# First steps of a LoRA feed-forward: high products ahead, gated rows in halves, A_down last

## The chip, the cores and the metric

The kernel runs on one core of a Trainium2 chip. The metric is the device time of one execution in microseconds (us). The core has five engines with queues of their own: TensorE (PE in the rows; PEld is its weight load), VectorE (DVE), ScalarE (ACT), GpSimd (POOL) and SyncE (SP, which here only issues DMAs). They meet through semaphores: an instruction raises one when it is done (`then_inc`), another waits until it has a value (`wait_ge`). Each queue runs in order, so an instruction that waits holds all behind it.

## The reference

For x of 32 sequences x 32 tokens x 512 the program computes two layers, each a "conditioner" and a feed-forward, with a residual:

```python
# layer 0, per sequence b with its expert id itok_B_2_6[b]
gate = x @ W_gate.T + 0.5 * (x @ A_gate[id].T) @ B_gate[id].T       # F = 1376, rank 16
up   = x @ W_up.T   + 0.5 * (x @ A_up[id].T)   @ B_up[id].T
act  = silu(gate) * up
down = act @ W_down.T + 0.5 * (act @ A_down[id].T) @ B_down[id].T    # back to 512
W_eff = U_top*relu(S_top*alpha+beta) @ Vh_top + U_tail*S_tail @ Vh_tail + U_r*S_r*relu(D) @ R @ Vh_r
x = x + down @ W_eff.T + bias
# layer 1: router over 8 experts, rank-16 LoRA of the top two, then an int8-like feed-forward
x = x + ffn_quantized(base(x) + 2 * lora_top2(x))
```

Only layer 0, up to its second feed-forward step, is touched.

## The kernel before

**Two numbers for one.** A float32 matmul is made of three products of rounded parts. Each operand is split in a high copy (`_hl[..., HI]`, a rounding copy on ScalarE, L559) and a low rest (raw minus high, a subtraction on VectorE, L907). TensorE then adds high x high, high x low and low x high in PSUM: `THREE`, L58. So every operand passes ScalarE, then VectorE, then TensorE.

**Steps.** The tokens are two halves (n = 0, 1) of 512. The 1376 rows of the hidden size are 11 tiles of 128, so layer 0 has 22 steps s = 11 n + f. A step is `gate_up` (L1337): 12 matmuls for gate, 6 of LoRA with B, 12 for up, 6 of LoRA; then silu on ScalarE (L645), times up on VectorE (L998, `act_raw`), the split of it (`act_hl`), and `down` (L1351): 6 matmuls with A_down (L1362) into the bank TD, 12 with W_down (L1369) into the banks 0 to 3. TensorE runs `gate_up(s + 1)` before `down(s)`.

**The first 44 us.** TensorE's order is written out (L1386 to L1413): warm-up, two of four effective-weight blocks (`w_eff`, L1299), a small product of the mix matrix (L1398, result `ps[TD]`, which ScalarE and VectorE copy to `c_hl`), step 0's 24 base matmuls for gate and up (L1326), `w_eff(2)`, x times the gathered A rows (`lora_in`, L1317), `w_eff(3)`, `delta` (L1308, reads `c_hl`), step 0's LoRA products with B (L1332), step 1's `gate_up`, step 0's `down`, step 2. The result of `lora_in` is masked so that each sequence keeps its own expert's rows (VectorE, four instructions at L977, to `tg_tmp`; the first two are the gate part, the last two the up part) and split to `tg_hl`; the LoRA products read that.

**The other queues.** ScalarE and VectorE go through the same steps, in `step` (L653, L1018): split the next step's gate/up weights and B rows, silu or product, then A_down (`ad_hl`), W_down (`wd_hl`) and `act_hl`. The A and B rows of a sequence's expert come by gathers that GpSimd issues one after the other (L472, L485), from a list that starts at once: A of gate and up, B of steps 0 and 1, A_down (L510), B of step 2, and so on. SyncE loads the rest; a buffer of weights is loaded again when both of its copies have been made (`load_wg`, L306; `load_wd`, L312), and these loads stand in order in one queue.

## Time and profile before

| | |
|---|---|
| median of 3 runs | 400.32 us (399.73 to 400.45) |
| profiled execution | 400.79 us |
| its span (first to last instruction) | 397.9 us |
| TensorE busy | 381.5 us, 96% |
| VectorE, ScalarE, GpSimd busy | 251.2, 187.7, 140.5 us |
| TensorE's granted clock | 0.9 or more of full speed in 39 of 40 slices |

The table says which engine is busiest over the whole span. It is an average: what an edit in the first tenth is worth is read from who waits for whom there, in the timelines of each engine, and from whether an engine waits later on.

### The profile page before, as it was taken

How to read it: one execution, taken by the hardware profiler on the slowest of the kernel's cores; microseconds unless marked ns; L12 is line 12 of the kernel's file. 1: busy time of each engine (PE TensorE's matmuls, PEld its weight loads, DVE VectorE, ACT ScalarE, POOL GpSimd, SP SyncE). 2: the span in 40 equal slices, each digit the busy share in tenths (PEclk: the TensorE clock that was granted, in tenths of full speed). 3: DMA queues.
4: the chain of work that ended last, by engine and by line, in shares of the span. 5: the costliest groups of instructions: out<-in, count | busy, mean ns of one | idle time of the engine just before them, and what ended most of it. 6: DMA issues, size and time to landing. Idle time of an engine off the chain costs nothing.

```text
span 397.9 us, 5993 instructions
## 1 busy us (share of the span) xinstructions
PE 381.5 (96%) x2029; PEld 302.9 (76%) x2029; DVE 251.2 (63%) x484; ACT 187.7 (47%) x313; POOL 140.5 (35%) x139
## 2 busy tenths in 40 slices
PE   7998999999999999999999999999989999999982
PEld 4687888888888988888888888889868874444442
DVE  5875844444454346756776666755574878989882
ACT  5544634333333244423454444642564547575760
POOL 2787877777301052200111130000000112757561
PEclk9999999999999999999999999999999999999998
DMA  7876644545333223732997796566378100113332
GB/s 285 283 229 239 212 138 146 160 158 161 115 105 105 81 79 110 238 112 92 311 284 210 204 234 162 106 107 224 126 186 203 73 0 2 37 44 93 89 90 80
DMA packets 48773, 58.84 MB, mean 148 GB/s; under 512 B 30305, under 2 KB 33147, under 8 KB 48623
## 3 DMA queue, kind: packets, MB, share of 16 engines
q1 hardware_dynamic: 43703, 47.15, 41.0%
q0 software_dynamic: 4320, 10.49, 8.6%
q10 hardware_dynamic: 728, 0.93, 0.7%
q8 instruction: 11, 0.18, 0.2%
q14 instruction: 11, 0.09, 0.1%
HBM read 50.02 MB, written 2.11 MB: 131 GB/s over the span
## 4 chain that ended last, share of the span: by engine, by line
PE 69%; DVE 12%; POOL 5%; ACT 5%; DMA 4%; issue 4%; SPq 0%; DVEq 0%; POOLq 0%; ACTq 0%
PE ps L1326 27%; PE ps L1369 15%; PE ps L1332 7%; PE ps L1484 5%; PE ps L1362 4%; PE ps L1438 3%; DVE hqs L1232 3%; ACT h_rnd L843 2%; DVE u_sb L1226 2%; POOL agu L472 2%; DVE g_sb L1223 2%; PE ps L1456 2%; PE ps L1379 1%; PE ps L1491 1%; DMA b_raw<-b_gu_dram,idx_all 1%
## 5 line engine op out<-in xcount | busy, mean ns | idle before, releaser
L1326 PE MATMUL ps<-x_hl,wg_hl 128*128 128x512 f32 x528 | 127.5, 391 | 0.7 <-DVE wg_hl L907 0.7
L1326 PEld LDWEIGHTS ps<-x_hl,wg_hl 128*128 128x128 f32 x528 | 97.6, 188 | 21.2 <-DVE wg_hl L907 1.6
L485 POOL DMA_INDIRECT b_raw<-b_gu_dram,idx_all x44 | 43.7, 994 | 95.5 <-DVE b_hl L907 84.9
L1369 PE MATMUL ps<-act_hl,wd_hl 128*128 128x512 f32 x264 | 64.0, 391 | 0.0
L1369 PEld LDWEIGHTS ps<-act_hl,wd_hl 128*128 128x128 f32 x264 | 48.2, 188 | 9.1
L998 DVE TENSOR_TENSOR act_raw<-ps,sil 128x512 f32<-128x512 f32 x22 | 15.2, 689 | 61.5 <-issue 37.3
L1332 PEld LDWEIGHTS ps<-tg_hl,b_hl 128*128 128x128 f32 x264 | 37.2, 190 | 4.5 <-issue 1.2
L1332 PE MATMUL ps<-tg_hl,b_hl 128*128 128x256 f32 x264 | 38.4, 282 | 0.8 <-DVE tg_hl L907 0.8
L527 POOL TENSOR_TENSOR qs<-qs,half 128x1 f32<-128x1 f32 x8 | 4.4, 551 | 89.0 <-DVE qs L1196 89.0
L559 ACT ACTIVATE act_hl<-act_raw 128x512 fp32r<-128x512 f32 x22 | 13.9, 632 | 44.8 <-DVE act_raw L998 44.8
L907 DVE TENSOR_TENSOR wg_hl<-wg_raw,wg_hl 128x1024 fp32r<-128x1024 f32 x22 | 26.9, 1224 | 12.6 <-ACT wg_hl L559 11.8
L536 POOL TENSOR_TENSOR g_sb<-g_sb,u_sb 128x459 f32<-128x459 f32 (+1 forms) x24 | 27.4, 1163 | 20.3 <-ACT g_sb L836 20.3
L691 ACT ACTIVATE nat<-nat,winv 128x512 f32<-128x512 f32 x22 | 14.7, 716 | 35.9 <-DVE winv L1010 35.9
L472 POOL DMA_INDIRECT agu<-a_gu_dram,idx_a x23 | 26.9, 1170 | 12.7 <-issue 6.7
L645 ACT ACTIVATE sil<-ps 128x512 f32<-128x512 f32 x22 | 12.9, 587 | 31.6 <-PE ps L1332 31.6
L472 POOL DMA_INDIRECT ad_raw<-a_d_dram,idx_a x24 | 25.0, 1040 | 7.3 <-issue 7.0
L1484 PE MATMUL ps<-wc_lo_hi,x_hl 128*128 128x512 f32 x96 | 23.8, 396 | 0.0
L1573 PE MATMUL ps<-wq_g,qt 128*128 128x459 bf16 (+1 forms) x96 | 22.6, 357 | 0.9 <-DVE g_sb L1223 0.9
L559 ACT ACTIVATE wg_hl<-wg_raw 128x1024 fp32r<-128x1024 f32 x22 | 23.0, 1045 | 0.2 <-DMA wg_raw<-w_gu_dram 0.2
L1438 PE MATMUL ps<-y_hl,we_hl 128*128 128x512 f32 x96 | 23.1, 394 | 0.0
L1573 PE MATMUL ps<-wq_u,qt 128*128 128x459 bf16 (+1 forms) x96 | 22.6, 358 | 0.0
L1362 PE MATMUL ps<-act_hl,ad_hl 128*128 128x256 f32 x132 | 19.6, 285 | 1.3 <-DVE act_hl L907 1.3
(173 smaller groups left out, 586.7 us busy)
## 6 DMA issues: line engine op xcount, KB each, us to landing
wg_raw<-w_gu_dram SPq DMA_DIRECT2D x22, 512.0 KB, 4.0
wd_raw<-w_d_dram SPq DMA_DIRECT2D x22, 256.0 KB, 2.7
nat<-w_nat_dram SPq DMA_DIRECT2D x11, 512.0 KB, 4.9
wdx<-w_nat_dram SPq DMA_DIRECT2D x11, 256.0 KB, 2.7
natd<-wd_nat_dram SPq DMA_DIRECT2D x4, 704.0 KB, 5.0
out_dram<-r_sb SPq DMA_DIRECT2D x7, 256.0 KB, 2.0
vu_raw<-w_vu_dram SPq DMA_DIRECT2D x3, 512.0 KB, 9.2
ws_b<-scale_scratch SPq DMA_DIRECT2D x2, 688.0 KB, 5.6
```

The costliest lines, as they stand in the source:

```text
L472: gp.indirect_dma_start(out=tile[:, b, :], out_offset=None, in_=a[table].rearrange("e p c -> (e p) c"), in_offset=bass.IndirectOffsetOnAxi ...
L485: gp.indirect_dma_start(out=b_raw[:, slot, g, :], out_offset=None, in_=a["b_gu"], in_offset=bass.IndirectOffsetOnAxis(ap=idx_all[:, f, 2 * ...
L536: nc.gpsimd.tensor_tensor(g_sb[:, slot, cols], g_sb[:, slot, cols], u_sb[:, slot, cols], ALU.mult).then_inc(h_made, 1)
L559: return nc.scalar.activation(o, i, ACT.Copy)
L907: return V.tensor_tensor(o, raw, hf(hi), ALU.subtract)
L1326: mm(bank[:], wg_hl[:, slot, w, gu * H + k * P:gu * H + (k + 1) * P], x_hl[n][:, v, k, :], start=(k == 0 and (w, v) == THREE[0]), stop=False)
L1332: last = mm(bank[:, g * GT:(g + 1) * GT], b_hl[:, slot, w, g, gu * P:(gu + 1) * P], tg_hl[:, n, v, gu, g * GT:(g + 1) * GT], start=False, ...
L1362: mm(ps[TD][:, g * GT:(g + 1) * GT], ad_hl[:, slot, w, g * P:(g + 1) * P], act_hl[:, slot, v, g * GT:(g + 1) * GT], start=(first and g == ...
L1369: last = mm(ps[m][:], wd_hl[:, slot, w, m * P:(m + 1) * P], act_hl[:, slot, v, :], start=(first and (w, v) == THREE[0]), stop=False)
L1438: last = mm(ps[m][:], we_hl[:, w, k, m * P:(m + 1) * P], y_of[n][:, v, k, :], start=(k == 0 and (w, v) == THREE[0]), stop=(k == KT - 1 and ...
L1484: mm(ps[CB[t]][:], x_hl[t // 4][:, w, k, (t % 4) * P:(t % 4 + 1) * P], wc_hl[v][:, k, :], start=(k == 0 and (w, v) == THREE[0]), stop=False)
L1573: last = mm(ps[(G_BANK, U_BANK)[gu][c]][:, 0:CH[c]], qt[:, t, k, :], wq(gu, k, slice(CO[c], CO[c] + CH[c])), start=(k == 0), stop=(k == KT ...
```

## The change

Three edits, all in the first two steps. TensorE does step 0's eight high x high products ahead of the mix product, and the other sixteen behind it. The split of the gated rows (`tg_hl`) is done in a gate half and an up half, on ScalarE and VectorE, with a count on the semaphores of two for each n; VectorE's split of step 1's weights goes behind it. In step 0 the split of A_down and its six matmuls go behind those of act and W_down.

```diff
             def tg_split(n):
-                act.wait_ge(tg_masked, 4 * (n + 1))
-                copy(tg_hl[:, n, HI], tg_tmp[:]).then_inc(tg_hi, 1)
+                for gu in range(2):
+                    act.wait_ge(tg_masked, 4 * n + 2 * gu + 2)
+                    copy(tg_hl[:, n, HI, gu], tg_tmp[:, gu]).then_inc(tg_hi, 1)
...
 
                 if not (isinstance(s, int) and s < 2):
                     act.wait_ge(down_done, s - 1)
-                ad_split(s, slot, f, n)
+                if not ad_behind:
+                    ad_split(s, slot, f, n)
                 wd_split(s, slot)
                 act_split(s, slot)
+                if ad_behind:
+                    act.wait_ge(ad_sp, 16 * AD_SP)
+                    act.wait_ge(ad_in[0], 16 * (HB - AD_SP))
+                    ad_split(s, slot, f, n)
 
             def bd_split(n):
...
-            act.wait_ge(ad_sp, 16 * AD_SP)
-            act.wait_ge(ad_in[0], 16 * (HB - AD_SP))
-            step(0, 0, 0, split_next=False, gate=False)
+            step(0, 0, 0, split_next=False, gate=False, ad_behind=True)
             step(1, 1, 0)
...
-                if n == 0:
-                    wg_split(1, 1)
-                dve.wait_ge(tg_masked, 4 * (n + 1))
-                dve.wait_ge(tg_hi, n + 1)
-                lo(tg_hl[:, n, LO], tg_tmp[:], tg_hl[:, n, HI]).then_inc(tg_lo, 1)
+                for gu in range(2):
+                    dve.wait_ge(tg_masked, 4 * n + 2 * gu + 2)
+                    dve.wait_ge(tg_hi, 2 * n + gu + 1)
+                    lo(tg_hl[:, n, LO, gu], tg_tmp[:, gu], tg_hl[:, n, HI, gu]).then_inc(tg_lo, 1)
 
             tg_split(0)
+            wg_split(1, 1)
             b_split(1, 1)
             for i in range(KT):
                 dve.wait_ge(we_hi, i + 1)
...
+            def ad_split(s, slot, f, n):
+                dve.wait_ge(ad_hi, s + 1)
+                lo(ad_hl[:, slot, LO, :].rearrange("p (b r) -> p b r", b=HB),
+                   ad_raw[:, n * HB:(n + 1) * HB, ds(f * RANK, RANK)],
+                   ad_hl[:, slot, HI, :].rearrange("p (b r) -> p b r", b=HB)).then_inc(ad_lo, 1)
+
+            def step(f, par, n, split_next=True, weights=True, ad_behind=False):
                 s, slot = n * FT + f, (n + par) % 2
                 if split_next:
                     wg_split(s + 1, 1 - slot)
                     b_split(s + 1, 1 - slot)
                 make_act(s, slot)
-                dve.wait_ge(ad_hi, s + 1)
-                lo(ad_hl[:, slot, LO, :].rearrange("p (b r) -> p b r", b=HB),
-                   ad_raw[:, n * HB:(n + 1) * HB, ds(f * RANK, RANK)],
-                   ad_hl[:, slot, HI, :].rearrange("p (b r) -> p b r", b=HB)).then_inc(ad_lo, 1)
+                if not ad_behind:
+                    ad_split(s, slot, f, n)
                 dve.wait_ge(wd_hi, s + 1)
                 lo(wd_hl[:, slot, LO, :], wd_raw[:, slot, :], wd_hl[:, slot, HI, :]).then_inc(wd_lo, 1)
                 dve.wait_ge(act_hi, s + 1)
                 lo(act_hl[:, slot, LO, :], act_raw[:], act_hl[:, slot, HI, :]).then_inc(act_lo, 1)
+                if ad_behind:
+                    ad_split(s, slot, f, n)
                 if n == 1 and weights and not (isinstance(f, int) and f < 2):
                     wq_max(f, par)
                     wq_round(f - 1, 1 - par)
@@ -1050,7 +1060,7 @@
                     dve.wait_ge(y_hi, KT * n + m + 1)
                     lo(y_of[n][:, LO, m, :], ps[m][:], y_of[n][:, HI, m, :]).then_inc(y_lo, 1)
 
-            step(0, 0, 0, split_next=False)
...
-            def gate_up_base(bank, slot, n, gu, first=False):
+            def gate_up_base(bank, slot, n, gu, first=False, terms=THREE):
                 for k in range(KT):
                     if first and k % 2 == 0:
                         pe.wait_ge(x_lo, k // 2 + 1)
-                    for w, v in THREE:
+                    for w, v in terms:
                         mm(bank[:], wg_hl[:, slot, w, gu * H + k * P:gu * H + (k + 1) * P], x_hl[n][:, v, k, :],
                            start=(k == 0 and (w, v) == THREE[0]), stop=False)
 
@@ -1341,15 +1351,24 @@
                 gate_up_base(ps[GATE], slot, n, 0)
                 pe.wait_ge(b_lo, s + 1)
                 if first:
-                    pe.wait_ge(tg_lo, n + 1)
+                    pe.wait_ge(tg_lo, 2 * (n + 1))
                 gate_up_lora(ps[GATE], slot, n, 0)
                 if not (isinstance(s, int) and s < 2):
                     pe.wait_ge(act_made, s - 1)
                 gate_up_base(ps[UP[slot]], slot, n, 1)
                 gate_up_lora(ps[UP[slot]], slot, n, 1)
 
+            def down_lora(s, slot, first, end):
+                pe.wait_ge(ad_lo, s + 1)
+                for g in range(2):
+                    for w, v in THREE:
+                        last = mm(ps[TD][:, g * GT:(g + 1) * GT], ad_hl[:, slot, w, g * P:(g + 1) * P],
+                                  act_hl[:, slot, v, g * GT:(g + 1) * GT], start=(first and g == 0 and (w, v) == THREE[0]),
+                                  stop=(end and g == 1 and (w, v) == THREE[-1]), skip_group_check=True)
+                return last
+
             def down(s, slot, n, first=False, end=False):
-                pe.wait_ge(ad_lo, s + 1)
+                lora_behind = first and not n
                 pe.wait_ge(wd_lo, s + 1)
                 pe.wait_ge(act_lo, s + 1)
                 if first:
@@ -1357,17 +1376,16 @@
                         pe.wait_ge(td_masked, n)
                     else:
                         pe.wait_ge(we_lo, KT)
-                for g in range(2):
-                    for w, v in THREE:
-                        mm(ps[TD][:, g * GT:(g + 1) * GT], ad_hl[:, slot, w, g * P:(g + 1) * P],
-                           act_hl[:, slot, v, g * GT:(g + 1) * GT], start=(first and g == 0 and (w, v) == THREE[0]),
-                           stop=(end and g == 1 and (w, v) == THREE[-1]), skip_group_check=True)
+                if not lora_behind:
+                    down_lora(s, slot, first, end)
                 for m in range(KT):
                     if first and n:
                         pe.wait_ge(x1_made, m + 1)
                     for w, v in THREE:
                         last = mm(ps[m][:], wd_hl[:, slot, w, m * P:(m + 1) * P], act_hl[:, slot, v, :],
                                   start=(first and (w, v) == THREE[0]), stop=False)
+                if lora_behind:
+                    last = down_lora(s, slot, first, end)
                 last.then_inc(down_done, 1)
 
             def lora_down(n):
@@ -1394,11 +1412,15 @@
             w_eff(0)
             w_eff(1)
 
+            pe.wait_ge(wg_hi, STEP0_TURN)
+            pe.wait_ge(x_hi, 2)
+            for gu, bank in ((0, ps[GATE]), (1, ps[UP[0]])):
+                gate_up_base(bank, 0, 0, gu, terms=THREE[0:1])
             pe.wait_ge(urs_ready, 1)
             mm(ps[TD][0:4, :], smalls[0:4, s_at["r"]], ur[:], start=True, stop=True).then_inc(cmix_ready, 1)
             pe.wait_ge(wg_lo, STEP0_TURN)
-            gate_up_base(ps[GATE], 0, 0, 0, first=True)
-            gate_up_base(ps[UP[0]], 0, 0, 1)
+            gate_up_base(ps[GATE], 0, 0, 0, first=True, terms=THREE[1:])
+            gate_up_base(ps[UP[0]], 0, 0, 1, terms=THREE[1:])
             w_eff(2)
             lora_in(0)
             w_eff(3)
@@ -1406,6 +1428,7 @@
             pe.wait_ge(b_lo, 1)
             pe.wait_ge(tg_lo, 1)
             gate_up_lora(ps[GATE], 0, 0, 0)
+            pe.wait_ge(tg_lo, 2)
             gate_up_lora(ps[UP[0]], 0, 0, 1)
             gate_up(1, 1, 0)
             down(0, 0, 0, first=True)
```

On TensorE, step 0's base matmuls (`x_hl` with `wg_hl`) around the mix product (`ur` with `consts`), before:

```order
L1398 MATMUL ps<-ur,consts 4x512 [waits urs_ready]
L1326 MATMUL ps<-x_hl_49,wg_hl 128x512 [waits x_lo,wg_lo]
L1326 MATMUL ps<-x_hl_49,wg_hl 128x512 x5
L1326 MATMUL ps<-x_hl_49,wg_hl 128x512 [waits x_lo]
L1326 MATMUL ps<-x_hl_49,wg_hl 128x512 x17
```

and now:

```order
L1336 MATMUL ps<-x_hl_49,wg_hl 128x512 [waits x_hi,wg_hi]
L1336 MATMUL ps<-x_hl_49,wg_hl 128x512 x7
L1420 MATMUL ps<-ur,consts 4x512 [waits urs_ready]
L1336 MATMUL ps<-x_hl_49,wg_hl 128x512 [waits x_lo,wg_lo]
L1336 MATMUL ps<-x_hl_49,wg_hl 128x512 x3
L1336 MATMUL ps<-x_hl_49,wg_hl 128x512 [waits x_lo]
L1336 MATMUL ps<-x_hl_49,wg_hl 128x512 x11
```

Eight of the 24 moved ahead of the mix product; they wait for the high copies alone. The same engine further on, from step 1's last LoRA products to step 2's first matmuls, before:

```order
L1332 MATMUL ps<-tg_hl,b_hl 128x256 x6
L1362 MATMUL ps<-act_hl,ad_hl 128x256 [waits act_lo,we_lo,wd_lo,ad_lo]
L1362 MATMUL ps<-act_hl,ad_hl 128x256 x5
L1369 MATMUL ps<-act_hl,wd_hl 128x512 x12
L1326 MATMUL ps<-x_hl_49,wg_hl 128x512 [waits silu_done,wg_lo]
```

and now:

```order
L1342 MATMUL ps<-tg_hl,b_hl 128x256 x6
L1385 MATMUL ps<-act_hl,wd_hl 128x512 [waits we_lo,act_lo,wd_lo]
L1385 MATMUL ps<-act_hl,wd_hl 128x512 x11
L1365 MATMUL ps<-act_hl,ad_hl 128x256 [waits ad_lo]
L1365 MATMUL ps<-act_hl,ad_hl 128x256 x5
L1336 MATMUL ps<-x_hl_49,wg_hl 128x512 [waits silu_done,wg_lo]
```

The wait for `ad_lo` now stands behind the twelve W_down matmuls. ScalarE, from the gated rows' copy to silu of step 1, before:

```order
L559 ACTIVATE tg_hl<-tg_tmp 128x1024 [waits tg_masked]
L559 ACTIVATE b_hl<-b_raw 128x512 [waits b_in1]
L645 ACTIVATE sil<-ps 128x512 [waits gate_ready]
L559 ACTIVATE we_hl<-ps 128x512 [waits we_ready] x4
L559 ACTIVATE ad_hl<-ad_raw 128x256 [waits ad_in0,ad_sp]
L559 ACTIVATE wd_hl<-wd_raw 128x512 [waits wd_in0]
L559 ACTIVATE act_hl<-act_raw 128x512 [waits act_made]
L559 ACTIVATE wg_hl<-wg_raw 128x1024 [waits wg_used,wg_in0]
L559 ACTIVATE b_hl<-b_raw 128x512 [waits b_in0]
L645 ACTIVATE sil<-ps 128x512 [waits act_made,gate_ready]
```

and now:

```order
L559 ACTIVATE tg_hl<-tg_tmp 128x512 [waits tg_masked] x2
L559 ACTIVATE b_hl<-b_raw 128x512 [waits b_in1]
L646 ACTIVATE sil<-ps 128x512 [waits gate_ready]
L559 ACTIVATE we_hl<-ps 128x512 [waits we_ready] x4
L559 ACTIVATE wd_hl<-wd_raw 128x512 [waits wd_in0]
L559 ACTIVATE act_hl<-act_raw 128x512 [waits act_made]
L559 ACTIVATE ad_hl<-ad_raw 128x256 [waits ad_in0,ad_sp]
L559 ACTIVATE wg_hl<-wg_raw 128x1024 [waits wg_used,wg_in0]
L559 ACTIVATE b_hl<-b_raw 128x512 [waits b_in0]
L646 ACTIVATE sil<-ps 128x512 [waits act_made,gate_ready]
```

The copy of A_down moved behind those of W_down and act; the copies for step 2 and the second silu are still behind it.

## Rows read from the trace of the kernel before

**Rows 1.** Busy us by stretch (column heads in its first line).
```profile
core 0: us, PE busy (x) PEld busy (x) DVE busy (x) ACT busy (x) POOL busy (x), PEclk, DMA share, GB/s
44.00:200.00 156.00, 156.00 (x828) 134.67 (x827) 80.28 (x123) 58.89 (x98) 60.88 (x59) 1.00 0.46 145
...
300.00:398.00 98.00, 87.85 (x493) 54.06 (x491) 76.28 (x182) 56.51 (x101) 40.53 (x39) 0.98 0.25 69
```

**Rows 2.** TensorE in order of time: start us, us, instruction, [idle before <-releaser].
```profile
12.07 1.02 PE L1398 MATMUL ps<-ur,consts 4*4 4x512 f32 x2
13.77 5.75 PE L1326 MATMUL ps<-x_hl,wg_hl 128*128 128x512 f32 x24 [0.68 <-DVE wg_hl L907]
19.35 2.88 PE L1299 MATMUL ps<-wg_hl 128*128 128x512 f32 x12
22.07 3.73 PE L1317 MATMUL ps<-x_raw,ag 128*128 128x128 f32 x32
25.56 2.98 PE L1299 MATMUL ps<-wg_hl 128*128 128x512 f32 x12
28.38 1.07 PE L1308 MATMUL ps<-c_hl,vr_hl 128*128 128x512 f32 x4
30.27 1.66 PE L1332 MATMUL ps<-tg_hl,b_hl 128*128 128x256 f32 x12 [0.82 <-DVE tg_hl L907]
31.99 3.00 PE L1326 MATMUL ps<-x_hl,wg_hl 128*128 128x512 f32 x12
...
40.45 0.95 PE L1362 MATMUL ps<-act_hl,ad_hl 128*128 128x256 f32 x6 [1.28 <-DVE act_hl L907]
...
43.96 2.88 PE L1326 MATMUL ps<-x_hl,wg_hl 128*128 128x512 f32 x12
...
54.32 2.88 PE L1326 MATMUL ps<-x_hl,wg_hl 128*128 128x512 f32 x12
```

**Rows 3.** ScalarE in order of time, same columns.
```profile
11.32 1.06 ACT L559 ACTIVATE wg_hl<-wg_raw 128x1024 fp32r<-128x1024 f32 x1 [0.22 <-DMA wg_raw<-w_gu_dram]
...
15.75 1.20 ACT L559 ACTIVATE c_hl<-ps 4x512 fp32r<-4x512 f32 x2 [0.98 <-DVE c_hl L952]
...
31.25 0.60 ACT L645 ACTIVATE sil<-ps 128x512 f32<-128x512 f32 x1 [1.94 <-PE ps L1332]
...
37.92 0.42 ACT L559 ACTIVATE ad_hl<-ad_raw 128x256 fp32r<-128x256 f32 x1 [4.12 <-DMA ad_raw<-a_d_dram,idx_a]
...
40.24 0.62 ACT L559 ACTIVATE b_hl<-b_raw 128x512 fp32r<-128x512 f32 x1
...
48.67 0.63 ACT L559 ACTIVATE b_hl<-b_raw 128x512 fp32r<-128x512 f32 x1 [2.39 <-DMA b_raw<-b_gu_dram,idx_all]
```

**Rows 4.** VectorE in order of time, same columns.
```profile
19.91 1.49 DVE L936 COPY ag<-agu 128x512 f32<-128x512 f32 x4 [1.04 <-DMA agu<-a_gu_dram,idx_a]
...
24.74 0.69 DVE L907 TENSOR_TENSOR b_hl<-b_raw,b_hl 128x512 fp32r<-128x512 f32 x1 [0.16 <-ACT b_hl L559]
25.91 1.78 DVE L977 TENSOR_TENSOR tg_tmp<-ps,consts 64x256 f32<-64x256 f32 x4 [0.48 <-PE ps L1317]
...
34.77 0.68 DVE L998 TENSOR_TENSOR act_raw<-ps,sil 128x512 f32<-128x512 f32 x1
...
40.43 1.23 DVE L907 TENSOR_TENSOR wg_hl<-wg_raw,wg_hl 128x1024 fp32r<-128x1024 f32 x1 [0.24 <-ACT wg_hl L559]
```

**Rows 5.** GpSimd's last gather of b for step 2, and such gathers' time to landing.
```profile
35.60 0.95 POOL L485 DMA_INDIRECT b_raw<-b_gu_dram,idx_all  x1 [0.30 <-issue]
...
DMA to landing us min/median/max: 2.8/3.5/4.5
```

**Rows 6.** SyncE's queue of DMAs, start us and us to issue.
```profile
39.66 0.34 SPq L315 DMA_DIRECT2D wd_raw<-w_d_dram  x1
40.41 0.35 SPq L310 DMA_DIRECT2D wg_raw<-w_gu_dram  x1
```

**Rows 7.** DMA engines by stretch: the last two columns are share and GB/s.
```profile
33.00:37.00 4.00, 4.00 (x22) 3.40 (x21) 2.45 (x5) 0.81 (x2) 2.99 (x4) 1.00 1.04 383
37.00:38.00 1.00, 1.00 (x6) 0.84 (x5) 0.00 (x0) 0.07 (x1) 0.79 (x1) 1.00 0.59 205
```

More of the change, by code:

```diff
@@ L492, in gather_bd @@
                 if n == 0:
-                    gp.wait_ge(tg_hi, NH)
-                    gp.wait_ge(tg_lo, NH)
+                    gp.wait_ge(tg_hi, 2 * NH)
+                    gp.wait_ge(tg_lo, 2 * NH)
                 else:
@@ L651, in act_split, with step @@
                 copy(act_hl[:, slot, HI, :], act_raw[:]).then_inc(act_hi, 1)
-            def step(f, par, n, split_next=True, gate=True):
+            def step(f, par, n, split_next=True, gate=True, ad_behind=False):
                 s, slot = n * FT + f, (n + par) % 2
@@ L971, in tg_split @@
                 if n:
-                    dve.wait_ge(tg_hi, n)
-                    dve.wait_ge(tg_lo, n)
+                    dve.wait_ge(tg_hi, 2 * n)
+                    dve.wait_ge(tg_lo, 2 * n)
                 for gu in range(2):
@@ L1016, in wq_round @@
                 V.tensor_scalar(nq[:, par, :], nat[:, par, :], ROUND, None, ALU.subtract).then_inc(nat_rounded, 1)
-            def step(f, par, n, split_next=True, weights=True):
+            def ad_split(s, slot, f, n):
[4 more added lines that the diff above has]
+            def step(f, par, n, split_next=True, weights=True, ad_behind=False):
                 s, slot = n * FT + f, (n + par) % 2
@@ L1051, in y_out @@
                     lo(y_of[n][:, LO, m, :], ps[m][:], y_of[n][:, HI, m, :]).then_inc(y_lo, 1)
-            step(0, 0, 0, split_next=False)
+            step(0, 0, 0, split_next=False, ad_behind=True)
             step(1, 1, 0)
```

## Prediction

> **What bounds the kernel now.** I read the busy time by stretch first: between 44 and 200 us TensorE is busy for all of its 156 us at a granted clock of 1.00, the higher of its two levels (2.4 GHz), and between 300 and 398 us for 87.85 of 98 us [rows 1]. So the middle of the program is one unbroken queue of matmuls, and what reaches 44 us earlier leaves 200 us earlier. All three parts of the change lie before 44 us, so TensorE's timeline of that stretch comes next [rows 2]. The reader is to see three places in it. The mix product (L1398, the only one of 4 rows) runs at 12.07 and the 24 gate/up matmuls of step 0 start at 13.77 after 0.68 us of idle. The gated LoRA products (L1332) start at 30.27 after 0.82 us. The first down step (L1362) starts at 40.45 after 1.28 us. Then ScalarE's and VectorE's timelines tell who was late [rows 3, 4], and GpSimd's and SyncE's what the DMAs do there [rows 5 to 7]. A "start of the next" below is a start plus the duration less 0.17 us, by which the modelled ends overlap (13.77 + 5.75 - 0.17 = 19.35) [rows 2].
>
> **Part 1, the eight high-by-high products first.** They need the high copies of the weights and of x, not the low ones. The later of these ends on ScalarE at 11.32 + 1.06 = 12.38 [rows 3]; with 0.12 us to get to TensorE, about what other handovers there take, the first of the eight starts at 12.50. One of the 24 takes (19.35 - 13.77) / 24 = 0.2325 us [rows 2], so the eight end at 14.36. The mix product takes its 1.02 - 0.17 = 0.85 us, to 15.21. The other 16 need VectorE's low copies, which were there for the start at 13.77; they run to 15.21 + 16 x 0.2325 = 18.93. Before it was 19.35: 0.42 us gained. No matmul is added. The price is that the mix product ends about 3.2 us later. ScalarE waits for it at L559 (c_hl), but that copy started at 15.75 because VectorE's clearing of c_hl came last [rows 3], and the product is out at 12.50 + 1.86 + 1.02 = 15.38. Hidden by 0.3 us; without that cover the delay would land on c_hl, which is needed only at 28.38 [rows 2].
> Does the 0.42 travel on? The effective-weight block (12 matmuls) takes 22.07 - 19.35 = 2.72 and would end at 21.65. The next one, L1317, needs VectorE's reordering of agu, which ends at 19.91 + 1.49 = 21.40 [rows 4]. It travels on, with 0.25 us to spare.
>
> **Part 2, the gated rows in two halves.** L1317 then ends at 21.65 + 3.49 = 25.14 for the next, and the two blocks behind it at 25.14 + 2.82 + 0.90 = 28.86 (22.07 to 25.56, 25.56 to 28.38, 28.38 + 1.07 - 0.17) [rows 2]. VectorE masks from 25.50 (before 25.91; its low copy of b for step 0 ends at 24.74 + 0.69 = 25.43, and that one hangs on a gather and does not move) [rows 4]. Two of the four masks are done after 0.89 us, at 26.4. ScalarE copies the gate half in about 0.63 us (a 128x512 copy [rows 3]), to 27.1; VectorE finishes the masks at 27.3 and takes the gate's low half in 0.69 us (a 128x512 subtraction [rows 4]) to 28.0. The up half is out at 28.7, where before the one low copy was in time only for 30.27. TensorE needs the gate half at 28.86 and the up half at 29.57. The stall goes whole: 29.28 to 30.27 is 0.99 us. What is late next is silu of step 0: it started at 31.25 for the gate products begun at 30.27, and the next matmuls waited for it until 31.99 [rows 2, 3]; that distance, 1.72 us, stays, so step 1 starts at 28.86 + 1.72 = 30.58. VectorE's low copy of step 1's weights, now behind these halves, takes 1.23 us [rows 4] and is out at 29.9, before 30.58 too. In the second half (n = 1) the two more instructions cost some 0.15 us each on ScalarE and VectorE, beside a busy TensorE [rows 1]; I count nothing.
>
> **Part 3, the first down step with A_down last.** ScalarE stood 4.12 us until 37.84 for the gather of ad_raw, and behind that wait were, in order, the copies of ad, wd, act, wg of step 2, b of step 2, and silu of step 1 [rows 3]. Now wd and act go ahead of it. They need act_raw, which VectorE began at 34.77 [rows 4] and now begins with silu's 1.4 us ahead, so it is out at 34.1; one low half of 0.69 us and another behind ScalarE's copy of act bring 35.5. Step 1 takes 31.99 to 39.00 (40.45 less its idle of 1.28 and 0.17), 7.01 us, so now it ends at 37.59, and the 12 W_down matmuls start without a wait. Before, it was 40.45: 1.45 us gone. The six A_down matmuls come last, at 40.3; ad's copies on the two engines take 0.42 us each after 37.92, so they are in time by 1.5 us. The whole step takes 43.96 - 40.45 = 3.51 [rows 2] and ends at 41.10.
>
> **The sum and its ceiling.** 0.42 + 0.99 + 1.45 = 2.86 us; step 2 starts at 41.10 for 43.96. But the copies of wg and b for step 2 and silu of step 1 are still behind ad on ScalarE. With the gather landing as before, wg's copy (1.06 us for step 0's) runs from 38.25 to 39.3 in the place that wd's had, and VectorE's part takes 1.23 more, so with two handovers step 2 could start at 40.75 [rows 3, 4]: 0.35 us of room. For b the trace shows only that it had landed by 40.24, where its copy ran with no idle [rows 3]. The last of its gathers began at 35.60, and these take 2.8, 3.5 or 4.5 us (minimum, median, maximum) [rows 5]: landing at 38.4 to 40.1. At 40.1, b's copy and silu (0.52 + 0.60 + 0.14) let TensorE start at 41.36, a loss of 0.26. And there is a side effect in SyncE's queue: the loads of wd (256 KB) and of wg (512 KB) for the coming steps went out at 39.66 and 40.41, on the copies that now end five us earlier [rows 6]. They move to about 34.7, into the time in which these gathers are in flight: the DMA engines are full from 33 to 37 us, at 383 GB/s, and at 0.59 of their time in 37 to 38 [rows 7]. 768 KB are 2.1 us at that rate. Bounds of this cost: nothing, if the gathers keep their share beside a queue that is full anyway, and 2.1 us, if every byte goes ahead of them. I take 0.15 us, near the lower end, as both loads stand in SyncE's queue behind x's second half (1 MB, L341) and step 2's wg (512 KB), which were on their way in that stretch already. Net gain 2.86 - 0.15 = 2.7.
> On exactly this the Trainium skill has a rule (DMA: Bandwidth & Descriptors, section Queues, rings and completion order): each DMA engine goes round robin between the queues that have work, a packet at a time. By it more bytes behind a full queue take nothing from the gathers, and the gain is the 2.7; if instead the gathers had to wait out the loads, it would be about 0.7. No row of before has these loads beside these gathers, so the trace doesn't decide it.
>
> **After that.** The gathers of b for step 3 land at 48.67 whatever TensorE does, since GpSimd issues without a pause there; silu of step 2 follows by about 49.9 [rows 3]. TensorE wants it at 54.32 - 2.86 = 51.46 [rows 2]. 1.5 us of room. From there TensorE never waits up to 200 us [rows 1], and the waits later are for results that start from it, so I carry the gain to the end in full.
>
> **The number.** The profiled execution took 400.79 us, 2.89 more than its span of 397.9. With 2.7 less it is 398.1; the median of the runs is 0.47 below the profiled one, 400.32, and gives 397.6.
>
> **The rivals.**
> (a) The loads and the gathers collide. ad_raw or b lands 0.7 to 2.1 us later; wg's low copy comes 2.9 us after ad (37.84 to 40.75), so TensorE starts step 2 at 41.5 to 42.9. Gain 1.1 to 2.5, time 397.8 to 399.2. For it: rows 7 show full engines. Against it: ad's gathers landed at 37.84 beside engines that were full of such loads already.
> (b) The gain is made and lost later: a part of the program behind 200 us is paced by something that does not start earlier, a DMA or GpSimd's queue, and not by TensorE. Time 399.5 to 400.3, no change. For it: TensorE is busy for only 87.85 of the last 98 us [rows 1]. Against it: those waits are for vector work on TensorE's own results.
> (c) Slower: the same collision delays b for step 2, place L559 on ScalarE, more than the ceiling holds. The new order loses once step 2 starts after 43.96, that is once ad lands after 41.05 or b after 42.7. Each 1 us beyond costs 1 us: a doubled price of 4.2 us for the 768 KB would give 40.75 + 4.2 = 44.95 and 401.3. Against it: 2.1 us of bytes can't do that without a slower DMA rate than any in rows 7.
> (d) The change doesn't do what it says, part 1 above all: if the mix product or agu's reordering decides, 0.42 is lost and the time is 398.0. It lies inside the forecast's own range.
>
> **Chances.** Forecast with (d), 397.0 to 398.1 (the sum without the 0.15 gives 397.5, and the runs of before spread by 0.7 us): 0.70. (a) 0.19, (b) 0.08, (c) 0.03. About 0.2% (0.8 us) is what a measurement of this kernel can tell from no change. (a) is faster for all its width, so faster is 0.89; the same is most of (b) and a little more, 0.08; slower 0.03. The range reaches over (a): 396.9 to 399.2.
>
> **What would show it.** Right: eight L1326 matmuls ahead of the mix product from about 12.5; no idle ahead of the LoRA products, which start near 28.9; step 1 near 30.6; the first W_down matmul near 37.6 with no idle; step 2 near 41.1 to 41.4; the same distance from there to the end of the span. SyncE's two loads near 35. Wrong: an idle of TensorE ahead of step 2 with b_hl, wg_hl or sil as its releaser (rival a), or a last stage that ends as late as before (rival b).

## The result, and the profile after

The changed kernel takes 397.91 us (median; 397.58 to 398.21), before 400.31 us: the ratio is 0.9942, 95% interval 0.993 to 0.9955. That is 2.4 us or 0.6% less, and the interval leaves out 1. Its profiled execution took 398.02 us with a span of 396.2 (the span is the time from the first to the last instruction). Against before's 400.79 and 397.9 that is 2.77 us less, of which 1.7 lie in the span and 1.07 outside it. The four executions of the changed kernel have spans of 395.7 to 396.4 us, and the 55 of before that the experiments below add have 397.3 to 398.8, median 397.8: in spans, too, the gain is 1.7 us. Four executions (one of before and one each of three variants) took 993 to 2202 us for no known reason and are left out of all numbers here.

TensorE's timeline of the changed kernel (start us, us, instruction, idle ahead of it and what ended it), against [rows 2]:

```profile
12.07 2.11 PE L1336 MATMUL ps<-x_hl,wg_hl 128*128 128x512 f32 x8
14.11 1.02 PE L1420 MATMUL ps<-ur,consts 4*4 4x512 f32 x2
15.06 3.94 PE L1336 MATMUL ps<-x_hl,wg_hl 128*128 128x512 f32 x16
18.84 2.88 PE L1309 MATMUL ps<-wg_hl 128*128 128x512 f32 x12
...
27.89 1.07 PE L1318 MATMUL ps<-c_hl,vr_hl 128*128 128x512 f32 x4
28.79 1.59 PE L1342 MATMUL ps<-tg_hl,b_hl 128*128 128x256 f32 x12
30.45 3.00 PE L1336 MATMUL ps<-x_hl,wg_hl 128*128 128x512 f32 x12
...
37.46 2.91 PE L1385 MATMUL ps<-act_hl,wd_hl 128*128 128x512 f32 x12
40.20 0.87 PE L1365 MATMUL ps<-act_hl,ad_hl 128*128 128x256 f32 x6
42.15 3.00 PE L1336 MATMUL ps<-x_hl,wg_hl 128*128 128x512 f32 x12 [1.07 <-ACT sil L646]
...
52.63 2.88 PE L1336 MATMUL ps<-x_hl,wg_hl 128*128 128x512 f32 x12
```

The three stalls are gone: the eight products run ahead of the mix product, the LoRA products start at 28.79 behind `delta` at once, and the W_down matmuls at 37.46. The down step is over for the next at 40.20 + 0.87 - 0.17 = 40.90. There is one new stall, 1.07 us ahead of step 2, which starts at 42.15 where [rows 2] has 43.96. So 1.81 us were gained up to there. Step 3 starts at 52.63 for 54.32, and the last matmul group, the final down step, at 387.31 for 388.97: the gain is carried, with 1.7 at the end.

ScalarE of the changed kernel tells what the new stall waits for, against [rows 3]:

```profile
10.95 1.06 ACT L559 ACTIVATE wg_hl<-wg_raw 128x1024 fp32r<-128x1024 f32 x1 [0.22 <-DMA wg_raw<-w_gu_dram]
...
15.54 1.20 ACT L559 ACTIVATE c_hl<-ps 4x512 fp32r<-4x512 f32 x2 [0.98 <-DVE c_hl L956]
...
38.42 0.42 ACT L559 ACTIVATE ad_hl<-ad_raw 128x256 fp32r<-128x256 f32 x1 [3.85 <-DMA ad_raw<-a_d_dram,idx_a]
...
40.89 0.63 ACT L559 ACTIVATE b_hl<-b_raw 128x512 fp32r<-128x512 f32 x1 [1.11 <-DMA b_raw<-b_gu_dram,idx_all]
41.43 0.58 ACT L646 ACTIVATE sil<-ps 128x512 f32<-128x512 f32 x1
```

A_down's rows are there at 38.42, half a microsecond later than before. The copy of b for step 2 had no idle ahead of it in before (40.24); here ScalarE waits 1.11 us for the gather, until 40.89, and silu of step 1 is behind that copy.

The two gathers of b for step 2 (from the view by tile, for 30 to 48 us), before and then changed:

```profile
DMA to landing us min/median/max: 2.8/3.2/3.6
```

```profile
DMA to landing us min/median/max: 5.1/5.7/6.2
```

SyncE's loads of wd and wg, against [rows 6], and the DMA engines, against [rows 7], both of the changed kernel:

```profile
34.58 0.35 SPq L315 DMA_DIRECT2D wd_raw<-w_d_dram  x1
35.33 0.35 SPq L310 DMA_DIRECT2D wg_raw<-w_gu_dram  x1
```

```profile
33.00:37.00 4.00, 4.00 (x23) 3.43 (x23) 2.20 (x4) 0.63 (x1) 3.08 (x4) 1.00 1.05 380
37.00:38.00 1.00, 1.00 (x9) 0.91 (x8) 0.00 (x0) 0.00 (x0) 0.69 (x2) 1.00 1.11 374
38.00:40.00 2.00, 2.00 (x11) 1.64 (x10) 0.53 (x2) 1.37 (x2) 1.70 (x2) 1.00 0.77 301
```

The two loads went out five microseconds earlier, as forecast. The engines, which were down to 0.59 at 37 to 38 in [rows 7], stay full until about 39.5, and the gathers beside them take up to 6.2 us to land instead of 3.6. The last of the two, issued at 34.66, is the one with 6.2; before, it had 2.8.

Each experiment below was timed beside before on the same chip, where before has medians of 400.3 to 400.5. Where two variants are compared, look at the intervals of their ratios to before, and at their spans.

### The profile page after: what moved, and what is told of

Its sections match the earlier page's. It is cut to its first block, busy times and chain, and to the rows that moved or that the text cites. A ratio compares the mean times of both kernels' runs of the same rounds, so it can differ in the third digit from the quotient of the medians.

```text
span 396.2 us, 5999 instructions
## 1 busy us (share of the span) xinstructions
PE 381.1 (96%) x2029; PEld 302.9 (76%) x2029; DVE 251.4 (63%) x486; ACT 188.3 (48%) x315; POOL 140.1 (35%) x139
## 4 chain that ended last, share of the span: by engine, by line
PE 68%; DVE 12%; POOL 7%; ACT 5%; issue 4%; DMA 3%; SPq 0%; DVEq 0%; POOLq 0%; ACTq 0%
PE ps L1336 28%; PE ps L1385 15%; PE ps L1342 7%; PE ps L1507 5%; PE ps L1365 4%; PE ps L1461 3%; DVE hqs L1242 3%; ACT h_rnd L847 2%; DVE u_sb L1236 2%; POOL agu L472 2%; POOL ad_raw L472 2%; DVE g_sb L1233 2%; PE ps L1479 2%; DMA b_raw<-b_gu_dram,idx_all 2%; PE ps L1397 1%
## 5 line engine op out<-in xcount | busy, mean ns | idle before, releaser
L472 POOL DMA_INDIRECT ad_raw<-a_d_dram,idx_a x24 | 24.2, 1009 | 7.3 <-issue 7.3
L1461 PEld LDWEIGHTS ps<-y_hl,we_hl 128*128 128x128 f32 x96 | 17.7, 188 | 3.5
```

What stands on the lines that cost most here:

```text
L472: gp.indirect_dma_start(out=tile[:, b, :], out_offset=None, in_=a[table].rearrange("e p c -> (e p) c"), in_offset=bass.IndirectOffsetOnAxi ...
L1461: last = mm(ps[m][:], we_hl[:, w, k, m * P:(m + 1) * P], y_of[n][:, v, k, :], start=(k == 0 and (w, v) == THREE[0]), stop=(k == KT - 1 and ...
```

## Which part is worth what

**Parts 1 and 2 without part 3.** The edit (on VectorE, too, `ad_behind=True` is taken out of step 0; lines between are left out):

```diff
-            step(0, 0, 0, split_next=False, gate=False, ad_behind=True)
+            act.wait_ge(ad_sp, 16 * AD_SP)
+            act.wait_ge(ad_in[0], 16 * (HB - AD_SP))
+            step(0, 0, 0, split_next=False, gate=False)
...
-                lora_behind = first and not n
+                lora_behind = False
```

> Parts 1 and 2 without part 3 (A_down first again, ScalarE's copy of A_down at its old place). Theory 1, the parts feed one wait: what parts 1 and 2 gain ends at the first down step, which waits for the gather of ad_raw whatever TensorE does. Step 1 starts near 30.5 us, the first down step near 40.5 as before, time 0 to 0.3 us below before (400.0 to 400.3). Theory 2, the sum of the prediction (0.42 + 0.99 for these two parts, each worth its stall): the first down step near 39.0 and a time 1.4 us below before, 398.9.

Measured: 401.26 us (399.48 to 402.98) for 400.49 of before, ratio 1.002 (1.0002 to 1.0039). Neither theory had it slower. TensorE around the first down step:

```profile
28.60 1.59 PE L1344 MATMUL ps<-tg_hl,b_hl 128*128 128x256 f32 x12
...
40.14 1.13 PE L1367 MATMUL ps<-act_hl,ad_hl 128*128 128x256 f32 x6 [2.75 <-DVE act_hl L913]
41.06 4.36 PE L1387 MATMUL ps<-act_hl,wd_hl 128*128 128x512 f32 x12
45.26 2.88 PE L1338 MATMUL ps<-x_hl,wg_hl 128*128 128x512 f32 x12
```

And its granted clock (the column ahead of the last two):

```profile
40.00:42.00 2.00, 1.86 (x9) 1.70 (x10) 1.75 (x3) 2.00 (x5) 1.70 (x2) 0.69 0.82 219
42.00:44.00 2.00, 2.00 (x6) 1.57 (x5) 2.00 (x5) 1.26 (x3) 1.39 (x3) 0.50 0.78 293
44.00:46.00 2.00, 2.00 (x10) 1.62 (x9) 1.08 (x2) 2.00 (x2) 1.70 (x2) 0.96 0.53 153
```

Theory 1 is right on the place: the LoRA products start 1.7 us earlier, and the down step at 40.14 for 40.45. What the two parts gained went into the stall for the same gather, which grew from 1.28 to 2.75 us. Behind it the granted clock is 0.50, 1.2 GHz, and the twelve W_down matmuls take 4.36 us for 2.91. The twelve executions fall in two groups: nine, the profiled one (0.991) among them, have a mean granted clock of 0.988 to 0.992 and spans of 398.9 to 401.1 us; three have 0.995 to 0.997 and 397.6 to 397.8, and 397.8 is the median span of before. So where the mean clock stays high the two parts are worth nothing, as theory 1 has it, and in the others they cost 1.1 to 3.3 us.

**Part 3 alone.** The edit undoes the others. Shown are part 1 and ScalarE's side of part 2; VectorE's split is one piece again too, with its split of step 1's weights ahead of it, and the counts of `tg_hi` and `tg_lo` are one for each n:

```diff
-            for gu, bank in ((0, ps[GATE]), (1, ps[UP[0]])):
-                gate_up_base(bank, 0, 0, gu, terms=THREE[0:1])
...
-                for gu in range(2):
-                    act.wait_ge(tg_masked, 4 * n + 2 * gu + 2)
-                    copy(tg_hl[:, n, HI, gu], tg_tmp[:, gu]).then_inc(tg_hi, 1)
+                act.wait_ge(tg_masked, 4 * (n + 1))
+                copy(tg_hl[:, n, HI], tg_tmp[:]).then_inc(tg_hi, 1)
```

> Part 3 alone (no high-by-high products ahead, gated rows in one piece, the weights' split of step 1 back at its place). Theory 1: the first down step starts without idle at 39.0 and step 2 near 42.5, 1.4 to 1.5 us below before (398.8), so that parts 1 and 2 add only 0.9 to 1.0 us on top of it, less than their 1.41. Theory 2, sums of separate stalls: also 1.45 here, but then parts 1 and 2 are worth 1.4 without it. Rival, the earlier loads of wd and wg collide with the gathers here too and hold step 2 to 43 or later: gain under 1.0.

Measured: 398.42 us (398.1 to 399.06), ratio 0.9953 (0.9939 to 0.9967). Step 2 starts behind the A_down matmuls with no idle:

```profile
38.92 2.91 PE L1384 MATMUL ps<-act_hl,wd_hl 128*128 128x512 f32 x12
41.67 0.88 PE L1364 MATMUL ps<-act_hl,ad_hl 128*128 128x256 f32 x6
42.38 2.91 PE L1335 MATMUL ps<-x_hl,wg_hl 128*128 128x512 f32 x12
```

So part 3 by itself is worth 2.07 us in time and 1.58 us at step 2's start. In spans (396.3 to 397.2 us, median 396.35) it is worth 1.45 of the 1.7, the number of its term; the other 0.6 us of its 2.07 lie outside the span. In time its interval overlaps that of all three parts (0.993 to 0.9955), so what parts 1 and 2 add is not separated from nothing. Its rival is right in part: the two loads go out at 36.05 and 36.80, the last gather of b takes 5.1 us and its copy waits until 40.67, but TensorE comes only at 42.38, so the collision holds nothing up.

**The halves of part 2 undone, parts 1 and 3 kept.** The edit is the second half of the diff above, on VectorE too (there the split of step 1's weights stays behind), with the counts of `tg_hi` and `tg_lo`.

> The changed kernel with the gated rows split in one piece again (VectorE's copy of step 1's weights stays behind it), parts 1 and 3 kept. The term of the prediction for the halves, 0.99 us, is a stall of TensorE ahead of step 0's LoRA products. Theory 1, step 2 waits for the gather of b anyway (step 2 began at 42.15 and 41.98 in two profiles of the changed kernel whose down steps ended 0.5 us apart): the LoRA products start at 29.7 to 30.0 instead of 28.8 to 29.3, the idle ahead of step 2 shrinks by the same, and the time is within 0.3 us of the changed kernel (397.9 to 398.2). Theory 2, the term is worth itself: 398.8 to 398.9.

Measured: 399.3 us (398.27 to 400.46), ratio to before 0.9975 (0.9962 to 0.9987). In its profile the idle of 0.82 us is back ahead of the LoRA products and step 2 starts at 42.03, where the changed kernel has 42.15:

```profile
29.83 1.67 PE L1340 MATMUL ps<-tg_hl,b_hl 128*128 128x256 f32 x12 [0.82 <-DVE tg_hl L910]
...
42.03 2.91 PE L1334 MATMUL ps<-x_hl,wg_hl 128*128 128x512 f32 x12
```

The profile is as theory 1 has it (span 395.9), the time is not: 1.4 us above the changed kernel, more than theory 2 as well. The twelve spans have a median of 396.4 us, 0.3 above the changed kernel's 396.1, which fits theory 1; about 1.0 us of the 1.4 lies outside the span (see below). The three longest times (400.0 to 400.5 us) have spans of 397.1 to 397.6; why stays open, as the profile is of the execution with the shortest span.

**Part 1 undone, parts 2 and 3 kept.**

```diff
-            for gu, bank in ((0, ps[GATE]), (1, ps[UP[0]])):
-                gate_up_base(bank, 0, 0, gu, terms=THREE[0:1])
-            gate_up_base(ps[GATE], 0, 0, 0, first=True, terms=THREE[1:])
-            gate_up_base(ps[UP[0]], 0, 0, 1, terms=THREE[1:])
+            gate_up_base(ps[GATE], 0, 0, 0, first=True)
+            gate_up_base(ps[UP[0]], 0, 0, 1)
```

> The changed kernel without part 1 (all 24 base matmuls of step 0 behind the mix product). Theory 1, as for the halves: nothing lost at the end, within 0.2 us of the changed kernel (397.9 to 398.1), since 0.42 us are less than the idle ahead of step 2. Theory 2, the term is worth itself: 398.3.

Measured: 398.35 us (398.03 to 398.42), ratio to before 0.9947 (0.9933 to 0.9961), 0.44 above the changed kernel, and 0.4 above it in spans (median 396.5). That is theory 2's number, though the intervals of the two overlap. But its profile shows TensorE waiting ahead of step 2 here too, so the 0.42 us can't have been decisive in that execution:

```profile
42.50 3.00 PE L1336 MATMUL ps<-x_hl,wg_hl 128*128 128x512 f32 x12 [0.77 <-ACT sil L646]
```

ScalarE's copy of b waited for the gather until 41.24, for 40.89 in the changed kernel; whether undoing part 1 or chance did that, the run doesn't tell. What part 1 is worth in the changed kernel stays open between 0 and 0.4 us.

## The new stall

**Loads held.** SyncE waits until ScalarE has copied b of step 2:

```diff
+            load_wg(2, 0, a["w_gu"][2])
+            sp.wait_ge(b_hi, 3)
+            load_wd(2, 0, a["w_d"][2])
-            step(2, 0)
```

> The changed kernel, and SyncE holds its load of wd for step 2 (and all behind it) until ScalarE has copied b of step 2. Theory 1, collision: these two loads, now at 34.6 and 35.3 us, slow the gather of b that landed at 40.9. Held back, b lands by 39.5, silu of step 1 ends by 40.7, step 2 starts near 41.0 without idle, and the time is about 1 us below the changed kernel (396.9). Rival, the gather is late of itself (GpSimd took 1.46 us for it instead of 0.95): it lands near 40.5 to 40.9 again, step 2 starts near 42, and the time is that of the changed kernel or higher by the later loads.

Measured: 397.39 us (397.1 to 398.2), ratio to before 0.9932 (0.9917 to 0.9946). The same two gathers, the stretch from 38 to 40 us, and TensorE:

```profile
DMA to landing us min/median/max: 3.7/3.9/4.1
```

```profile
38.00:40.00 2.00, 2.00 (x11) 1.67 (x11) 0.57 (x2) 1.62 (x3) 1.41 (x2) 1.00 0.16 51
```

```profile
12.57 2.14 PE L1338 MATMUL ps<-x_hl,wg_hl 128*128 128x512 f32 x8 [0.59 <-ACT wg_hl L561]
...
41.52 2.91 PE L1338 MATMUL ps<-x_hl,wg_hl 128*128 128x512 f32 x12
```

The gathers take 4.1 us at most for 6.2, although GpSimd's instruction took 1.46 us here too; the DMA engines are at 0.16 from 38 to 40 us for 0.77; and TensorE has no idle ahead of step 2. The collision is shown, and the rival, a gather late of itself, is out. The other profiles agree: with the two loads late, the last gather of b takes 2.8 to 4.0 us in six of them and 4.9 in the seventh; with the loads beside it 5.1, 5.3, 5.6 and 6.2, and in the two others ScalarE's copy of b waits until 5.9 and 7.0 us after its issue.

In time it gives 0.5 us, half of what was expected, and the intervals of the two ratios overlap, as the spans do (395.3 to 396.4 for 395.2 to 396.4, medians 395.6 and 396.1). The profiled execution shows a whole microsecond at the place itself: it began its first gate/up product 0.5 us later (12.57 for 12.07), and from that product to step 2 it took 28.95 us, the changed kernel 30.08 and 29.55.

**Silu of step 1 and wg of step 2 ahead of the wait for ad_raw**, loads early. ScalarE's lines are shown; VectorE has `wg_split(2, 0)` ahead of A_down's low copy, and step 1 leaves out what was done:

```diff
                 if ad_behind:
+                    silu(1)
+                    wg_split(2, 0)
                     act.wait_ge(ad_sp, 16 * AD_SP)
```

> The changed kernel, and ScalarE does silu of step 1 and the copy of wg for step 2 ahead of its wait for ad_raw (VectorE the low copy of wg ahead of that of A_down). The loads stay early. Theory 1: TensorE's 1.07 us of idle ahead of step 2 is ScalarE's order, b's gather standing in front of silu; with silu ahead step 2 starts at 40.9 to 41.0 without idle and the time is 1.0 to 1.2 us below the changed kernel (396.7 to 396.9). Rival: the stall only moves on, to the LoRA products of step 2 or to step 3, which need b: then the time stays within 0.3 us of the changed kernel.

Measured: 397.8 us (397.3 to 398.2), ratio to before 0.9937 (0.9924 to 0.995), as the changed kernel.

```profile
40.88 0.98 PE L1370 MATMUL ps<-act_hl,ad_hl 128*128 128x256 f32 x6 [0.32 <-DVE ad_hl L914]
41.70 2.91 PE L1341 MATMUL ps<-x_hl,wg_hl 128*128 128x512 f32 x12
```

```profile
37.62 1.06 ACT L559 ACTIVATE wg_hl<-wg_raw 128x1024 fp32r<-128x1024 f32 x1 [2.37 <-DMA wg_raw<-w_gu_dram]
38.59 0.40 ACT L559 ACTIVATE ad_hl<-ad_raw 128x256 fp32r<-128x256 f32 x1
41.88 0.63 ACT L559 ACTIVATE b_hl<-b_raw 128x512 fp32r<-128x512 f32 x1 [2.89 <-DMA b_raw<-b_gu_dram,idx_all]
```

The gather of b lands only at 41.88 and no longer holds step 2, which starts at 41.70 for the 40.9 to 41.0 expected. wg of step 2, though, comes at 37.62, its copies on ScalarE and VectorE hold those of A_down behind them, and 0.32 us of idle stand ahead of the A_down matmuls. The time is that of the rival, and the stall moved on, though not to the places that it named.

**The changed kernel again**, beside the next ones:

> The changed kernel once more, beside the others of this set, so that they are compared on one chip. It should take 397.9 (2.4 us below before). If its step 2 starts after an idle of 0.7 to 1.3 us that silu or b's copy ends again, the collision seen in its first profile is a regular one; without idle it was chance.

Measured: 397.92 us (397.04 to 398.23), ratio 0.9937 (0.9919 to 0.9954).

```profile
12.43 2.11 PE L1336 MATMUL ps<-x_hl,wg_hl 128*128 128x512 f32 x8 [0.33 <-ACT wg_hl L559]
...
41.98 2.99 PE L1336 MATMUL ps<-x_hl,wg_hl 128*128 128x512 f32 x12 [0.44 <-ACT sil L646]
```

The idle ahead of step 2 is 0.44 us, behind silu again. TensorE came there 0.47 us later than in the first profile and step 2 started 0.17 earlier: the gather sets that start, not TensorE. The idle is smaller than the 0.7 to 1.3 us expected, but the collision is a regular one: it is there in both profiles.

**Silu ahead and loads held**, the version that the runs pointed to (silu is taken out of step 1, and SyncE waits ahead of `load_wd(2, ...)`):

```diff
                 if ad_behind:
+                    silu(1)
                     act.wait_ge(ad_sp, 16 * AD_SP)
...
+            sp.wait_ge(b_hi, 3)
```

> The changed kernel with the loads held as in the run before, and with silu of step 1 ahead of ScalarE's wait for ad_raw (wg of step 2 stays behind). Theory, both causes of the idle ahead of step 2 are gone: no idle from the first high-by-high product to 200 us, 0.5 to 1.0 us below the changed kernel (397.0 to 397.4). Rival, holding alone gave all of it: the same as holding alone, and silu's place is worth nothing.

Measured: 397.61 us (397.2 to 398.13), ratio to before 0.993 (0.9911 to 0.9948), outside the 397.0 to 397.4 expected. In the profile nothing stands ahead of step 2, which starts at 41.01, 28.83 us behind the first gate/up product, and the span is the shortest of all, 394.9 us. But the time is only 0.3 below the changed kernel, which the intervals don't separate, and the spans have the median of holding alone (395.5 and 395.6 us). So the rival has it: silu's place is worth nothing once the loads are held.

## The granted clock

**Parts 1 and 2, the gap filled** with eleven matmuls that add nothing to the output:

```diff
             gate_up(1, 1, 0)
+            for i in range(11):
+                mm(ps[TD][:], x_hl[0][:, HI, 0, 0:P], x_hl[0][:, HI, 0, :], start=True, stop=True)
             down(0, 0, 0, first=True)
```

> Parts 1 and 2 without part 3, and eleven extra matmuls (high x by itself, to the bank TD, whose content the first down product replaces) in TensorE's idle ahead of the first down step; they add nothing to the output. Theory, the granted clock: in parts 1 and 2 alone TensorE stood 2.75 us and the clock was 0.50 afterwards, 42 to 44 us, so twelve W_down matmuls took 4.36 us for 2.91 in the changed kernel. With the gap filled they take 2.9, the time falls by 1.3 to 1.8 us to about 399.7 and its spread (399.5 to 403.0) closes. Rival, the slower matmuls come of memory traffic by the loads that land then: then they take over 4 us again and the time stays near 401.3.

Measured: 400.19 us (399.52 to 400.91) for 401.26 (399.48 to 402.98) unfilled; ratio to before 0.9993 (0.9983 to 1.0004). TensorE, and the stretch from 42 to 44 us:

```profile
37.63 2.68 PE L1437 MATMUL ps<-x_hl 128*128 128x512 f32 x11
41.66 0.95 PE L1367 MATMUL ps<-act_hl,ad_hl 128*128 128x256 f32 x6 [1.35 <-DVE act_hl L913]
42.45 2.89 PE L1387 MATMUL ps<-act_hl,wd_hl 128*128 128x512 f32 x12
```

```profile
42.00:44.00 2.00, 2.00 (x13) 1.76 (x12) 2.00 (x3) 1.53 (x4) 1.55 (x2) 1.00 1.00 297
```

The W_down matmuls take 2.89 us although A_down's gather was later here and 1.35 us of idle are left. The clock is 1.00 there, and the DMA engines move 297 GB/s at a share of 1.00, no less than the 293 GB/s at 0.78 of the unfilled kernel. The cause of the 4.36 us is the clock, and not the loads. All twelve executions have a mean clock of 0.995 or more and spans of 397.7 to 399.1 us: the group with the lower clock is gone. The gain of 1.07 is under the 1.3 to 1.8 expected.

**The kernel before, filled** with five such matmuls:

> The kernel before with five such matmuls in its idle of 1.28 us ahead of the first down step. In its one profile the granted clock stayed 1.00 after that idle. Theory A, that holds for its other executions too: filled, the time is that of before within 0.3 us. Theory B, some executions of before fall to the lower clock there, and part of the 2.4 us that the changed kernel gained is that the gap is gone (its step 2 started only 1.8 us earlier): then filling makes before faster by 0.4 to 0.8 us and its spread smaller.

Measured: 399.54 us (399.1 to 400.55), ratio 0.9981 (0.9969 to 0.9993): 0.8 to 0.9 us faster than before, as theory B has it. But the gain is not where B puts it. The spans are 397.3 to 398.7 us, median 397.7, beside 397.3 to 398.8, median 397.8, of before: filling made nothing inside the span shorter. What lies outside it is 1.80 to 1.88 us in all eleven executions, and 2.59 in the median of before. B's share of the 2.4 us is not seen; A has it right inside the span.

**Before, profiled twice more:**

> The kernel before, profiled a second time, for the granted clock behind its idle ahead of the first down step. If some of its executions fall to the lower clock there, as the filled kernel's 0.8 us suggest, one of two more profiles may show a clock under 1.00 between 40 and 46 us and first down-step matmuls over 3 us; if none does, the 0.8 us have another source or the fall is rarer.

> The kernel before, profiled a third time, for the same reason and with the same two outcomes.

The second profile is 402.6 us long, the third 400.46. Of the second:

```profile
40.94 1.23 PE L1362 MATMUL ps<-act_hl,ad_hl 128*128 128x256 f32 x6 [1.82 <-DVE act_hl L907]
41.97 4.25 PE L1369 MATMUL ps<-act_hl,wd_hl 128*128 128x512 f32 x12
46.06 2.90 PE L1326 MATMUL ps<-x_hl,wg_hl 128*128 128x512 f32 x12
```

```profile
42.00:44.00 2.00, 2.00 (x6) 1.61 (x6) 2.00 (x5) 1.26 (x4) 1.70 (x2) 0.50 0.99 325
44.00:46.00 2.00, 2.00 (x8) 1.58 (x8) 1.08 (x3) 2.00 (x3) 1.46 (x2) 0.79 0.60 168
```

Here A_down's gather was later, TensorE stood 1.82 us, and the clock fell to 0.50: twelve matmuls in 4.25 us, step 2 at 46.06. The third has 1.27 us of idle, a clock of 1.00 and step 2 at 43.64. So before can fall there. But this execution has a span of 400.0 us, and none of the 55 timed ones of before is above 398.8. Five of them have a mean clock of 0.990 or 0.991, as this one (0.991), with spans of 397.5 to 398.5; where in those the clock fell, nothing here shows. A fall like this one is rare, and not in the median.

## What lies around the span

The page's queue q8, which its line calls instruction, has 11 or 12 packets in the span. That number goes with the time less the span in all fourteen profiles:

| q8 packets in the span | time less span, us | profiles |
|---|---|---|
| 12 | 1.80 to 1.88 | changed (two), parts 1 and 2 (plain and filled), loads held, silu and wg ahead, before filled, part 1 undone |
| 11 | 2.55 to 2.96 | before (three), part 3 alone, halves undone, silu ahead with loads held |

The two lines of the page, before and changed:

```profile
q8 instruction: 11, 0.18, 0.2%
```

```profile
q8 instruction: 12, 0.20, 0.2%
```

It is not a fixed property of a kernel, though. The timed executions have their spans on record too, and one kernel can have both values. Part 3 alone has 2.55 us in the profiled execution and 1.80 to 1.88 in the five others; silu ahead with loads held has 2.90 in the profiled one and 1.80 to 1.83 in the others. Before has 1.79 to 1.86 in eight of 55 and 2.07 to 3.09 in the rest, median 2.59; halves undone has 1.87 to 3.04, median 2.82. The changed kernel has 1.80 to 1.88 in all ten, and so has before with nothing but five matmuls added in all eleven. So of the 2.4 us between the medians about 0.7 lie outside the span, and they come from how often the larger value occurs, which no part of the change was meant to touch. That the packets cause it is only a correlation, and what decides it was not tried.

## Why the prediction was right, step by step

The time, 397.91 for 397.6, is in the range and in the forecast's own, and the sign is right. But the sum behind it has one term that was far too small, and it gets back what it lost from outside. That the number fits so well is luck.

- Part 1 (0.42): the timeline shows 19.35 - 18.84 = 0.51, but most of it because the high copies were ready at 12.01 rather than 12.38, so that the eight started at 12.07 for 12.50. From their start to the next block it took 6.77 us for the 6.43 forecast (the eight 2.04 for 1.86, the mix product 0.95 for 0.85, the sixteen 3.78 for 3.72), which from 12.50 would have left 0.08. Over all profiles `w_eff(2)`, the block behind, starts at 18.98 us in the median of the eight with part 1, and at 19.33 in that of the six without: the term is 0.35, near its forecast. The mix product was hidden behind c_hl's clearing, as forecast (c_hl's copy at 15.54, released by VectorE).
- Part 2 (0.99): the stall is gone, and the chain of starts came out to 0.1 us: 28.79 for 28.86, step 1 at 30.45 for 30.58, with silu as the next late one.
- Part 3 (1.45): W_down at 37.46 for 37.59, no idle, A_down in time. Right.
- The step that failed is the collision's price. It was put at 0.15 us inside bounds of 0 and 2.1. Measured, step 2 starts at 42.15 and 41.98 for a floor by TensorE of 40.90 and 41.37: 1.07 and 0.44 us of idle, and none in either kernel with the loads held. This is rival (a), which had 0.19: its collision, its sign (an idle ahead of step 2 with sil as releaser), its window for step 2 (41.5 to 42.9) and its time (397.8 to 399.2) came, though by the gather of b and silu behind it, and not by wg's low copy, from which it was worked out. Forecast and rival overlap from 397.8 to 398.1, so the time alone can't tell them apart; the profile can. The reasons for the low value, that the gathers keep their share beside a queue that is full anyway, failed in its "anyway": the queue was emptying at 37 to 38 us [rows 7], and the last gather, begun at 34.66 and 35.10 in the two profiles of the changed kernel, was still in flight then. The loads kept the engines full some 2 us longer, and the gather took 6.2 and 5.6 us for 3.7 and 4.0 in the two profiles with the loads held: 1.6 to 2.5 us more, about the upper bound that the prediction had. What was drawn from the rule of the Trainium skill (DMA: Bandwidth & Descriptors, Queues, rings and completion order), that the gathers lose nothing, the trace does not bear out: 6.2 us for the last gather, and 3.7 with the loads held, are against it. Whether the turns between the queues are as the rule says, no run here shows.
- Ceiling of the sum: that each part is worth its stall holds only while nothing fixed in time stands behind. Parts 1 and 2 together are worth nothing without part 3, and part 3 alone gives 2.07 of the 2.4 (1.45 of 1.7 in spans). The prediction added the three terms and checked the ceiling for the sum, but not the order in which they count: most of what parts 1 and 2 brought was swallowed by the gather of b.
- "I carry the gain to the end in full": 1.81 at step 2, 1.69 at step 3, 1.66 at the last group. Right within 0.15; rival (b) fell, as TensorE's busy 156 of 156 us went on.
- The 2.89 us by which the time is more than the span were taken as fixed. They were 1.82 in the changed kernel's profile. With 2.89 the profiled execution would have taken 399.1 us for 398.02. In medians: the span fell by 1.7 us and not by 2.7, and with the 2.6 us that before has outside its span the changed kernel would have taken 398.7 us. That is outside the forecast's own range (397.0 to 398.1), inside rival (a)'s and inside the stated range. So the forecast number owes 0.7 to 1 us to a term that it didn't have.

## What to carry to other kernels

Before terms are added, put every transfer that starts by its own clock on the same time line and ask which of them is behind each stall; a stall taken away ahead of such a transfer is worth nothing and can cost, if the engine then stands longer and its clock falls. When an earlier result releases a buffer, the load that fills it goes out earlier too: look for what is in flight just then, and hold the load by a wait on what it would delay, as one line on SyncE did here. And compare spans as well as times, of many executions and not of the profiled one alone: two executions of one kernel can differ by a microsecond outside the span.

## What the runs showed of the hardware that was not expected

- Behind idles of 2.75 and 1.82 us TensorE was granted 0.50 of its clock, 1.2 GHz, from 42 to 44 us (12 matmuls of 128x512 in 4.36 and 4.25 us for 2.91). Behind idles of 1.27, 1.28 and 1.35 us at the same place, and of 1.07 ahead of step 2, it stayed at 1.00.
- The last gather of b for step 2 took 2.8 to 4.9 us in the seven profiles that show its landing with no other loads issued beside it, and 5.1 to 6.2 in the four with 768 KB of other loads issued within 2 us of it.
- The time less the span is 1.80 to 1.88 us with 12 packets of q8 in the span and 2.55 to 2.96 with 11 (fourteen profiles), and it changes between executions of one kernel (1.79 to 3.09 us for before).
